# Splitting the experts' weights inside the periods of the cross-attention

## The reference

```python
x = x + xattn(layernorm(x), ctx, mask)   # 16 heads, 1601 keys for each of the 32 batch elements; masked softmax
x = x + attn(layernorm(x))               # self-attention over 64 tokens, causal; the values are scaled by a gate
x = x + ffn(layernorm(x))                # 8 experts (256 -> 2*704 -> 256, silu(a)*g), the best 2 for each token
```

## Time and profile before

| | us |
|---|---|
| median of 3 executions | 1889.3 (1888.94 to 1891.74) |
| the profiled execution | 1884.02 |
| its span | 1882.2 |
| a period of the cross-attention | 40.3 |
| self-attention block | 1330.3 to 1577.9 of the span: 247.6 |
| TensorE, VectorE, ScalarE, GpSimd busy over the span | 1736.2, 1387.1, 1307.0, 1293.4 |

### The profile page before, as it was taken

One profiled execution on the slowest core, in us unless ns is written; L12 is line 12 of the kernel. 1 busy time (PEld: TensorE's weight loads), 2 busy tenths in 40 slices (PEclk: granted clock), 3 DMA queues, 4 the chain that ended last, 5 costly groups with the idle time before them and its releaser, 6 DMA issues. The chain is left out here.

```text
span 1882.2 us, 59167 instructions
## 1 busy us (share of the span) xinstructions
PE 1736.2 (92%) x24673; PEld 1146.0 (61%) x24673; DVE 1387.1 (74%) x3579; ACT 1307.0 (69%) x1610; POOL 1293.4 (69%) x669
## 2 busy tenths in 40 slices
PE   6899999999999999999999999999778993699996
PEld 3566666666666666666666666666534672588885
DVE  7788888888888888888888888788766566544443
ACT  5588788888878888878888878888664442233332
POOL 3488888898888888898898888888652100243442
PEclk9999999999999999999999999999898785799998
DMA  8544445444445544445554545554166674688884
GB/s 274 157 119 121 128 113 156 130 127 112 131 117 151 136 129 112 131 117 146 138 132 111 132 117 142 134 138 104 51 215 203 202 236 148 241 248 254 267 245 119
DMA packets 170923, 290.83 MB, mean 155 GB/s; under 512 B 56162, under 2 KB 138466, under 8 KB 170434
## 3 DMA queue, kind: packets, MB, share of 16 engines
q1 hardware_dynamic: 163170, 276.83, 50.6%
q0 software_dynamic: 7488, 10.23, 2.7%
HBM read 169.80 MB, written 33.16 MB: 108 GB/s over the span
## 5 line engine op out<-in xcount | busy, mean ns | idle before, releaser
L420 POOL TENSOR_TENSOR pl<-pT,ph 128x1024 f16<-128x1024 f32 x416 | 881.7, 2132 | 188.4 <-ACT ph L462 188.2
L679 DVE CUSTOM_DVE_ANT_0 junk<-ring,mbias 128x804 bf16<-128x804 f32 x496 | 491.5, 991 | 155.7 <-issue 150.1
L460 ACT ACTIVATE pT<-score,small 128x1024 f32<-128x1024 f32 (+1 forms) x416 | 464.5, 1117 | 68.0 <-PE score L485 34.0
L462 ACT ACTIVATE ph<-score,small 128x1024 f16<-128x1024 f32 (+1 forms) x416 | 464.5, 1117 | 0.0
L883 PE MATMUL ring<-cp,wkp 128*128 128x402 f16 x1536 | 309.0, 338 | 10.2 <-DVE kst L758 3.3
L894 PE MATMUL ring<-wvp,cp 128*128 128x256 f16 (+1 forms) x2496 | 306.3, 274 | 2.9 <-DVE v L664 1.7
L894 PEld LDWEIGHTS ring<-wvp,cp 128*128 128x128 f16 (+1 forms) x2496 | 233.7, 99 | 78.4 <-issue 21.8
L623 POOL TENSOR_TENSOR cp<-cx,cp 128x804 f16<-128x804 f32 x128 | 252.9, 1996 | 21.5 <-ACT cp L792 21.5
L800 ACT ACTIVATE kh<-ring,small 128x402 f16<-128x402 f32 x256 | 155.2, 606 | 154.9 <-PE ring L883 154.9
L908 PE MATMUL ring<-kh,qm 32*128 32x402 f16 x992 | 253.1, 334 | 4.9 <-DVE mx L679 0.3
L507 PE MATMUL o_acc<-v,pl 128*128 128x33 f16 (+1 forms) x3328 | 240.2, 178 | 0.0
(11 more groups left out here) (243 smaller groups left out, 2098.5 us busy)
## 6 DMA issues: line engine op xcount, KB each, us to landing
cx<-in_ctxT SPq DMA_DIRECT2D x32, 1601.0 KB, 6.7
w1p<-wsp SPq DMA_DIRECT2D x24, 1408.0 KB, 8.0
kst<-kh SPq DMA_DIRECT2D x256, 100.5 KB, 2.9
msk<-in_mask SPq DMA_DIRECT2D x64, 400.2 KB, 5.5
kst<-kh SPq DMA_DIRECT2D x256, 99.6 KB, 2.5
wsp<-w_parts SPq DMA_DIRECT2D x24, 704.0 KB, 5.8
w2p<-wsp SPq DMA_DIRECT2D x24, 640.0 KB, 4.3
kst<-kl SPq DMA_DIRECT2D x128, 100.5 KB, 2.7
```

Source lines behind the costliest of these rows:

```text
L420: pool.tensor_tensor(pl[:, u].rearrange("p h q -> p (h q)"), pT[:, u], ph[:, u].rearrange("p h q -> p (h q)"), ALU.subtract).then_inc(pl_r ...
L460: act.activation(pT[0:n, u].rearrange("k (h a q) -> k a h q", a=2, q=S), scored, ACT.Exp, bias=lift[0:n, 0:1], scale=SSCALE)
L462: act.activation(ph[0:n, u].rearrange("k h (a q) -> k a h q", a=2), scored, ACT.Exp, bias=lift[0:n, 0:1], scale=SSCALE).then_inc(exp_done, 1)
L679: dve.tensor_tensor_reduce(junk[:, n % 2], made[:, :, 0:KW], mbias[:, j, 2 * KW * half:2 * KW * half + 2 * KW].rearrange("p (c k) -> p c k ...
```

## The change

All 24 pieces are split in the periods 0 to 24 of the cross-attention. In period b, HI of piece b is last in ScalarE's list, LW0 of piece b-1 stands between X12 and X13 in VectorE's (one instruction for a piece: `LPARTS` is 1), and SyncE stores piece b-1 and loads piece b ahead of the second half of the keys. There is one buffer in place of two: the next load waits for LW of the piece before, HI for the store before. The buffers lie over `xn`, `pack` and `bv`, which the lead-in alone uses (the first load waits until they are spent); the small tiles of the self-attention move there later. The lists of the self-attention lose WL, HI, LW and WS and stand in a new order throughout; in it N0 of VectorE comes ahead of ZN0, SK1 ahead of SQ1. SyncE's wait for all stores moves from the experts' block to `load_constants` in period 30. The instructions of a piece are the same as before.

```diff
-ACT_ORDER = steps("KH0 E0 KH1 ... E10 CH3 E11 E12")
+ACT_ORDER = steps("KH0 E0 KH1 ... E10 CH3 E11 E12 HI")
 DVE_ORDER = steps("KL0 N KL1 ... X10 X11 KL7 X12 "
-                  "X13 VH3 X14 VL3 X15 SH VH4 SPR VL4 VH5 VH6 VL5 VL6 MP")
+                  "LW0 X13 VH3 X14 VL3 X15 SH VH4 SPR VL4 VH5 VH6 VL5 VL6 MP")
...
+            w_whole = nc.alloc_sbuf_tensor_at("w_whole", [P, WP], F32, offset=at_spent)
+            w_parts = nc.alloc_sbuf_tensor_at("w_parts", [P, 2, WP], F16, offset=at_spent + 4 * WP)
...
+                    def load_whole(q):
+
+                        e, k = q // PIECES, q % PIECES
+                        if q == 0:
+                            sp.wait_ge(q_kept, DC * NCH)
+                            sp.wait_ge(blocks_ready, 2 * NCH)
+                            sp.wait_ge(wp_ready, 3)
+                            sp.wait_ge(bv_added, 1)
+                        after(sp, w_low, LPARTS * q)
+                        if k < DC:
+                            sp.dma_start(w_whole[:], a["w1T"][e, P * k:P * k + P]).then_inc(w_in, 16)
+                        else:
+                            sp.dma_start(w_whole[:, 0:(FT - 1) * D].rearrange("p (t d) -> p t d", d=D),
+                                         a["w2T"][e, 0:(FT - 1) * P].rearrange("(t p) d -> p t d", p=P)).then_inc(w_in, 16)
+                            sp.dma_start(w_whole[:, (FT - 1) * D:WP],
+                                         a["w2T"][e, (FT - 1) * P:F].rearrange("r (h f) -> (r h) f", h=2)).then_inc(w_in, 16)
+
+                    def store_parts(q):
+
+                        sp.wait_ge(w_low, LPARTS * q + LPARTS)
+                        sp.dma_start(wsp[q // PIECES, q % PIECES], w_parts[:]).then_inc(w_out, 16)
+
                     def load_constants():
+
+                        sp.wait_ge(w_out, 16 * E * PIECES)
...
                             load_mask(b + 2)
                             load_block_queries(b + 2, j)
+                        if 1 <= b <= E * PIECES:
+                            store_parts(b - 1)
+                        if b < E * PIECES:
+                            load_whole(b)
                         stack_keys(b + 1, 1 - j, 1)
                         shift_queries(b + 1, 1 - j)
...
+                            elif kind == "LW" and 1 <= b <= E * PIECES:
+                                cols = slice(WSLICE * n, WSLICE * n + WSLICE)
+                                dve.wait_ge(w_high, b)
+                                dve.scalar_tensor_tensor(w_parts[:, 1, cols], w_whole[:, cols], WSCALE, w_parts[:, 0, cols], ALU.mult, ALU.subtract).then_inc(w_low, 1)
...
+                            elif kind == "HI" and b < E * PIECES:
+                                act.wait_ge(w_in, 16 * (b + 1 + (b + 1) // PIECES))
+                                after(act, w_out, 16 * b)
+                                act.activation(w_parts[:, 0], w_whole[:], ACT.Copy, scale=WSCALE).then_inc(w_high, 1)
...
-                    for j in range(2):
-                        sp.wait_ge(w_out[j], 16 * (E * PIECES // 2))
                     sp.wait_ge(te_ready, 1)
```

More of the change, by code:

```diff
@@ L75 @@
 WP = 2 * F
+LPARTS = 1
+WSLICE = WP // LPARTS
 HOT = 4
@@ L137 @@
 HT = TILES // 2
-SELF_PE = steps("ZS0 ZS1 ZS2 ZW0 ZS3 ZS4 ZW1 ZS5 ZW2 ZS6 ZW3 X0 X1 ZW4 ZS7 V0 V1 ZW5 ZS8 Q0 Q1 ZS9 ZW6 ZS10 ZW7 ZW8 V2 "
[7 rows of a table removed]
-SELF_ACT = steps("ZE0 ZE1 ZE2 ZE3 ZE4 XN0 XN1 XN2 XN3 ZE5 XC0 XC1 XN4 ZE6 ZE7 ZE8 QH0 QH1 ZE9 ZE10 ZE11 ZE12 KH0 XN5 "
[6 rows of a table removed]
-SELF_POOL = steps("ZL0 ZL1 ZL2 ZL3 ZL4 BO0 ZL5 ZL6 ZL7 ZL8 ZL9 ZL10 ZL11 ZL12 BO1 ZA0 BO2 HG0 BO3 HW0 PR0 HM0 VG0 VG1 "
-                  "VG2 VG3 HG1 HW1 PR1 HM1 VG4 VG5 VG6 VG7")
-SELF_DVE = steps("ZN0 ST0 ST1 ST2 ST3 ST4 N0 ST5 ST6 ST7 ST8 ST9 ST10 ST11 ST12 ST13 ST14 N1 VV0 HS0 VV1 HS1 QL0 QL1 "
[8 rows of a table removed]
-SELF_SP = steps("RO0 SQ0 WL0 WL1 SK0 RO1 WL2 WS0 WL3 WS1 SQ1 WL4 WS2 SK1 WL5 WS3 SH0 SH1 SQ2 WS4 WL6 WL7 SH2 SH3 WS5 "
[3 rows of a table removed]
+SELF_PE = steps("ZS0 ZS1 ZS2 ZS3 X0 ZW0 ZW1 X1 ZS4 V0 V1 ZS5 ZW2 Q0 V2 V3 ZS6 Q1 ZS7 ZW3 ZW4 ZW5 K0 K1 ZW6 ZS8 ZS9 X2 "
[7 rows of a table added]
+SELF_ACT = steps("ZE0 ZE1 XN0 XN1 XN2 XN3 ZE2 XC0 XC1 ZE3 ZE4 XN4 XN5 XN6 XN7 QH0 ZE5 QH1 ZE6 ZE7 KH0 KH1 ZE8 XN8 XN9 "
[5 rows of a table added]
+SELF_POOL = steps("ZL0 ZL1 BO0 ZL2 ZL3 ZL4 BO1 ZL5 ZL6 ZL7 ZL8 BO2 ZL9 ZL10 ZL11 ZL12 HG0 ZA0 HW0 PR0 BO3 HM0 VG0 VG1 "
+                  "VG2 VG3 HG1 HW1 PR1 HM1 VG4 VG5 VG6 VG7")
+SELF_DVE = steps("ST0 ST1 ST2 ST3 N0 ZN0 ST4 ST5 ST6 ST7 ST8 ST9 ST10 ST11 N1 VV0 HS0 VV1 ST12 ST13 HS1 ST14 VV2 QL0 "
[7 rows of a table added]
+SELF_SP = steps("RO0 SQ0 SK0 SK1 SH0 RO1 SQ1 SH1 SH2 SK2 SH3 SH4 SQ2 SK3 SH5 SH6 SH7 SH8 SQ3 SH9 AS0 SH10 XS0 AS1 SH11 "
+                "XS1 SH12 SH13 SH14 AS2 XS2 SH15 AS3 XS3")
 SELF_USES = [use for use in SELF_PE if use[0] in ("X", "Q", "K", "V", "T", "A", "TU")]
@@ L197, in program @@
         ident = sb("ident", [P, P])
-        xn = sb("xn", [P, 4, D])
         ln_st = sb("ln_st", [P, TILES, 6])
@@ L204, in program @@
         mixed = sb("mixed", [P, TILES, 3 * E])
+        at_spent = -(-nc.sbuf_base // 32) * 32
+        xn = sb("xn", [P, 4, D])
         xn_d = nc.dram_tensor("xn_d", (TOK, D), F32).ap()
@@ L250, in mark @@
                 return -(-nc.sbuf_base // 32) * 32
+            at_first = mark()
+            pack = sb1("pack", [P, PACK])
+            wk, wv, wq = (pack[:, DC * D * n:DC * D * n + DC * D].rearrange("p (c d) -> p c d", c=DC) for n in range(3))
+            bk, bq, sel_q = (pack[:, 3 * DC * D + DC * n:3 * DC * D + DC * n + DC] for n in range(3))
+            bv = sb1("bv", [P, D])
+            w_whole = nc.alloc_sbuf_tensor_at("w_whole", [P, WP], F32, offset=at_spent)
+            w_parts = nc.alloc_sbuf_tensor_at("w_parts", [P, 2, WP], F16, offset=at_spent + 4 * WP)
             at_consts = mark()
+            assert at_spent + 8 * WP <= at_consts
             cx = sb1("cx", [P, DC, NKP])
@@ L258, in program @@
             at_soon = mark()
[L259 to L262, removed]
             cp = sb1("cp", [P, 2, 2, DC, NKP], F16)
@@ L332, in room @@
                 return place
-            consts, late, soon, last = (room(at, end) for at, end in ((at_consts, at_keys), (at_keys, at_soon),
-                                                                      (at_soon, at_mbias + 2 * NKP), (at_last, at_end)))
+            first, consts, late, soon, last = (room(at, end) for at, end in ((at_first, at_consts), (at_consts, at_keys), (at_keys, at_soon),
+                                                                             (at_soon, at_mbias + 2 * NKP), (at_last, at_end)))
             wq2, wk2, wo2 = (consts(n, [P, DC, D]) for n in ("wq2", "wk2", "wo2"))
@@ L345, in program @@
             turner = consts("turner", [P, P])
[L347 to L350, removed]
+            mv1, mvh, mv2 = (first(n, [P, TILES, 2]) for n in ("mv1", "mvh", "mv2"))
+            inv1, invh, inv2 = (first(n, [P, TILES]) for n in ("inv1", "invh", "inv2"))
+            off1, offh, off2 = (first(n, [P, TILES]) for n in ("off1", "offh", "off2"))
+            st_x, st_h, st_y = (first(n, [P, TILES, 6]) for n in ("st_x", "st_h", "st_y"))
             xt = soon("xt", [P, 2, DC, CH])
@@ L355, in program @@
             hd = soon("hd", [P, TILES, DP])
[L356 to L359, removed]
+            drift, pre, gate = first("drift", [P, 2, TILES]), first("pre", [P, TILES, GW]), first("gate", [P, 2, TILES])
+            top2 = first("top2", [P, 2, STRIP])
+            mtc = first("mtc", [STRIP, 4, P], F16)
+            rs2 = first("rs2", [P, H])
             pT2 = late("pT2", [P, 2, H, S])
@@ L377, in program @@
             first2_in, consts2_in, rows2_in = sem("first2_in"), sem("consts2_in"), sem("rows2_in")
-            w_in, w_out = [sem(f"w_whole_in{j}") for j in range(2)], [sem(f"w_parts_out{j}") for j in range(2)]
+            w_in, w_out = sem("w_whole_in"), sem("w_parts_out")
             w_high, w_low = sem("w_high_parts"), sem("w_low_parts")
@@ L986, in stack @@
                                              src[STRIP * r:STRIP * r + STRIP]).then_inc(done, 16)
-                    def load_whole(q):
-                        e, k, j = q // PIECES, q % PIECES, q % 2
-                        after(sp, w_low, q - 1)
-                        if k < DC:
-                            sp.dma_start(w_whole[:, j], a["w1T"][e, P * k:P * k + P]).then_inc(w_in[j], 16)
-                        else:
-                            sp.dma_start(w_whole[:, j, 0:(FT - 1) * D].rearrange("p (t d) -> p t d", d=D),
-                                         a["w2T"][e, 0:(FT - 1) * P].rearrange("(t p) d -> p t d", p=P)).then_inc(w_in[j], 16)
-                            sp.dma_start(w_whole[:, j, (FT - 1) * D:WP],
-                                         a["w2T"][e, (FT - 1) * P:F].rearrange("r (h f) -> (r h) f", h=2)).then_inc(w_in[j], 16)
                     for kind, n in SELF_SP:
@@ L1023, in _ @@
```

(12 more changed lines are left out.)

8 lines of the change are left out of this document (1 added, 7 removed), and 41 rows, old and new, of tables (SELF_ACT, SELF_DVE, SELF_PE, SELF_SP).

## The result

The changed kernel takes 1966.9 us (median of 4 runs, 1961.0 to 1973.4), the kernel before 1889.1 on the same chip (4 runs, 1885.7 to 1891.7): ratio 1.041, interval 1.037 to 1.045. It is slower by 4%. The forecast was 1952, with 1915 to 2015 as its range.

What follows compares the result with a forecast made beforehand. TensorE was taken to bound the cross-attention, chains between engines the self-attention. Late shift +79, slower issues +10 and self-attention -26 gave +63 on the median 1889.3: 1952 us, range 1915 to 2015.

Steps and rivals of the forecast that it cites:

- The mechanism and its size: Cross-attention periods: SyncE's store waits for LW, so shift and S0 come 3.1 or 3.7 us later; 79 us in all.
- signs of being wrong: Period near 40.8 us, clock in periods under 1.00, LW's mean 2 us or more, self-attention shrinking much more than 26.
- Slower issues: Cross-attention periods: SyncE's issues get slower among more DMA traffic, 0.4 us per period, 10 us in all.
- rival B: Cross-attention: the clock falls in the new stall at S0, 72 us more over 24 periods, 2024 us; chance 0.12.
- The self-attention, -26: Self-attention stage: without the split's LW, HI and issues, and in a new order, it gets 26 us shorter.
- the floor: Self-attention: the gain is at most 46 us, when TensorE's 201.1 us of work become the bound.
- HI at nothing: Cross-attention periods: HI, last in ScalarE's order, costs nothing; without cover it would cost up to its 1.37 us.
- C: Cross-attention periods: LW meets a GpSimd instruction after all, 2.0 us in each of 24, 48 us, 2000 us; chance 0.10.
- D: Cross-attention: SyncE's delay does not reach S0, periods pay only LW's 12 us, 1875 us; chance 0.12.

Runs made afterwards that it cites:

- e1: The changed kernel with VectorE's whole LW moved from between X12 and X13 to between X4 and X5: 1860.9 us, 0.985 of the kernel before.
- e6: e1 plus scratch fills on VectorE where LW stood in the changed kernel, which SyncE awaits ahead of its store: 1990.2 us, 1.055 of the kernel before.
- e2: The changed kernel with twelve extra matmuls, their result overwritten, ahead of TensorE's wait for the shift in periods 2 to 25: 1920.0 us, 1.016 of the kernel before.
- e8: e1 with LW cut into two halves of 704 columns, ahead of X2 and ahead of X5: 1844.2 us, 0.977 of the kernel before.
- e4: The kernel before with the split's steps struck from the self-attention's lists, the scratch copy of the weights filled once: 1920.9 us, a total spoilt by that fill.
- e7: The changed kernel with the self-attention's old lists, struck of the split's steps; the split stays in the periods: 1995.6 us, 1.059 of the kernel before.
- e5: The changed kernel with LW cut into four pieces of 352 columns, ahead of X0, X2, X4 and VH2: 1894.3 us, 1.003 of the kernel before.
- e9: e1 with the whole LW ahead of X2 and not ahead of X5: 1857.5 us, 0.983 of the kernel before.

## Why the prediction came out as it did

**The mechanism and its size: right.** The step "SyncE's store waits for LW and stands ahead of the 12 transfers, the shift and S0" is shown by e1 and e6 together. The forecast loop was 43.4 us from S0 to S0; the period in the windows above that kept its clock has 43.44 from shift to shift and 43.53 from S0 to S0. Over all periods the forecast had 79 us, and e2 less e8 gives 80, some 3.5 of them the clock in e2's two rounds (23 of TensorE's 24 waits at S0 in the changed kernel sum to 74.3).

The range held, but two of the prediction's own signs of being wrong came up: the clock in the periods was under 1.00 (0.95), and the self-attention shrank by much more than 26 us. The first cost 43 us more than forecast and the second 19 us less; that 1952 came as near to 1966.9 as it did is in part luck.

**Slower issues, 10 us: they did not come.** From the first late stack to the shift it was 8.52 us before and 8.67 after in the two periods shown, and over the 24 periods 8.75 on the mean before and 8.77 after. With no stall the split costs 0.2 us a period (e8), 5 us in 24, and these are not the stacks' issues.

**The clock, the term that was missing.** The step that failed is in rival B: "against: it lies between the two", a fall only where the stall comes near 3.74 us, at 3 us a period. It was given 0.12, and it came true behind 22 of 24 stalls, at 1.8 us a period on the mean (e2): 43 us where B in full had 72. The size was off since the clock was mostly back sooner than the 6 us it had, after 4.2 on the mean: the period shown above lost 2.7 us (46.14 less 43.44). Of the split periods behind a stall, the 21 whose clock fell span 44.6 to 47.4 us, and the two whose clock did not took 43.4 and 44.6. The two stalls read in the self-attention could not tell where the edge lies; there is no such edge in the stall's length (below). The Trainium skill (TensorE: Matmul & The Clock Gate, HAM oscillation — how this bites in real kernels) tells of a loop that loses its clock in each round by one wait for DMA. The trace agrees in 22 of 24 rounds. But that loop waits some 3 to 5 us a round, and the stall forecast here was 2.6 to 3.2, so "by it B would be the rule" said more than the page does.

**The self-attention, -26 against -44.9.** The term was mis-sized, and by its parts: what I counted was mainly the work struck out (10 for the issues, 8 for LW, 3 for the last LW at the end, 2 for traffic), and that, measured by e4, is 15.4 and not 23. The new order I had at 3, at the head alone; it measured 28 (e7). I named TensorE's 201.1 busy us as the floor, at -46. That was no floor: the number held the low clock of 0.83, and fell to 181 when the clock rose. The total came near that bound by another way.

**HI at nothing, C, D.** HI took 1.37 us in ScalarE's pause and nobody waited for it. C did not happen: LW took 1.62 us 24 times. The margin was thin: the prediction had LW start 0.04 us behind the end of GpSimd's instruction, and in the trace it starts 0.04 us ahead of that end; e5 shows what a worse place costs. D did not happen either. Where its condition is made true, with no delay at S0, e1 is at 1861 and e8 at 1844 and not at 1875; most of the difference is the self-attention (1889 + 12 - 45 would be 1856).

**Outside the forecast.** The experts' part took 3.2 us more and the start 2.5; in that last part the runs e1 to e9 have 301.4 to 306.9 us, and at the start 69.5 to 73.1, where no experiment changed anything. No cause is shown.

The sum of what was missed: clock +43, stall +1, self-attention -19, slower issues -10, the 0.2 us a period of e8 +5, other +6: 26 us over the 1947 that was forecast for the profiled execution, which took 1973.4.

## What to carry to other kernels

In all these traces SyncE's queue issues in the order in which it is written. When a store is put into it, what counts is not the store's own 0.4 us but what it waits for, and who stands behind it; place the producer so early that the store finds it done. (The other remedy, the store and the load behind the shift, was not tried.) A stall of some 3 us on TensorE in each round of a loop has to be priced with the clock behind it, here 1.8 us on 3.3; and where the stall can't be removed, idle matmuls in it can win that part back (47 us in e2). Small waits have to be watched too: in e1 one of 0.95 us was followed by a fallen clock in 5 of 24 periods. A busy time taken at a low clock is no lower bound of a stage. Cutting a VectorE instruction finer to fit the holes can make it dearer (1.62 to 5.1 us in e5), if each piece can meet an instruction of GpSimd: look at both engines' pauses.

## What the hardware showed that I had not expected

Whether the clock falls does not follow from the length of the stall. Three S0 of the changed kernel, with the wait ahead of each:

```profile
988.02 0.61 PE L482 MATMUL score<-delta,mbias 64*128 64x512 bf16 x2 [2.31 <-issue]
...
1033.64 0.39 PE L482 MATMUL score<-delta,mbias 64*128 64x512 bf16 x2 [3.41 <-issue]
...
1123.73 0.39 PE L482 MATMUL score<-delta,mbias 64*128 64x512 bf16 x2 [2.74 <-issue]
```

After 2.31 us of waiting the work ran at 1.2 GHz from its first matmul; after 3.41 us it ran at 2.4 GHz all through; after 2.74 us it began at 2.4 and the clock fell behind it (0.63 over the next 3 us). A second stall that left the clock at 1.00 had 3.25 us. And e1's waits of 0.95 us, a third as long, were followed by a fallen clock five times. What tells these apart is not in the rows that I read.

The mutual exclusion of VectorE and GpSimd stretched a VectorE instruction of 0.51 us nearly fivefold, to 2.46, and which of the two engines paid was set by tenths of a microsecond in their start: in e5, pieces that began 0.14 to 0.30 us ahead of a GpSimd instruction took 0.52 us and the GpSimd instruction 2.20 to 2.37; those that began 0.28 to 0.36 us behind the start of one of 2.13 us took 2.15 to 2.22 us.
